# A graph network of 14 hops: the gathered edges' one-hot moves from the streaming side of the matrix product to the stationary side, in two halves of the array's columns

## What is computed

```
agg = segment_sum(h[src] * w[:, None], dst, num_segments=N)   # 14 times
out = agg @ W (+ h @ Wr) + bias ; layernorm / relu / residual
```

## Time and profile before

| what | value |
|---|---|
| time, median of 3 runs | 6878.76 us (6877.93 to 6886.88) |
| the profiled execution | 6887.01 us, span 6885.1 us |
| PE busy | 6183.2 us, 90% of the span |
| POOL busy | 4719.0 us, 69% |
| DVE busy | 2158.9 us, 31% |
| mean granted PE clock | 0.975 |

### The profile page before, as it was taken

One profiled execution on the slowest core, in us unless ns is written; L12 is line 12 of the kernel. 1 busy time (PEld: TensorE's weight loads), 2 busy tenths in 40 slices (PEclk: granted clock), 3 DMA queues, 4 the chain that ended last, 5 costly groups with the idle time before them and its releaser, 6 DMA issues.

```text
span 6885.1 us, 79487 instructions
## 1 busy us (share of the span) xinstructions
PE 6183.2 (90%) x27391; PEld 3701.9 (54%) x27592; DVE 2158.9 (31%) x8268; ACT 309.1 (4%) x843; POOL 4719.0 (69%) x4959
## 2 busy tenths in 40 slices
PE   0499752999999999989999999999999999999998
PEld 0399521655555555545655555555555555655555
DVE  8644720223322221212222233222223322222244
ACT  0000000000000000000000000000000000000000
POOL 0677777566666667667677676776767767677676
PEclk9999976999999999999999999999999999999999
DMA  9475332666666767778888888888888888888887
GB/s 359 173 310 224 97 97 77 202 195 203 181 195 184 213 199 217 218 247 288 283 290 290 294 296 288 280 286 279 296 295 289 291 286 280 285 292 291 300 295 231
DMA packets 582180, 1703.64 MB, mean 247 GB/s; under 512 B 163490, under 2 KB 325467, under 8 KB 479392
## 3 DMA queue, kind: packets, MB, share of 16 engines
q1 hardware_dynamic: 316850, 1337.88, 56.9%
q0 software_dynamic: 157584, 240.14, 12.2%
q10 hardware_dynamic: 107388, 120.98, 5.0%
HBM read 1476.43 MB, written 223.40 MB: 247 GB/s over the span
## 4 chain that ended last, share of the span: by engine, by line
PE 61%; POOL 15%; DMA 13%; issue 11%; DVE 0%; POOLq 0%; SPq 0%; ACT 0%; ACTq 0%; DVEq 0%
PE pwide L1055 33%; PE pwide L1051 16%; PE pstep L1084 9%; POOL ring_f L655 7%; POOL counts L629 6%; DMA ring_f<-table,f_src 5%; DMA counts<-lane_val,lane_idx 3%; DMA counts<-zz 3%; POOL weights L629 1%; PE pwide L1142 1%; DMA weights<-lane_val,lane_idx 1%; PE pwide L1141 0%; PE pwide L1100 0%; PE pwide L1137 0%; PE pwide L1065 0%
## 5 line engine op out<-in xcount | busy, mean ns | idle before, releaser
L655 POOL DMA_INDIRECT ring_f<-table,f_src x3492 | 3322.0, 951 | 1518.3 <-issue 916.0
L1055 PE MATMUL pwide<-room,acc 128*128 128x512 f32 (+1 forms) x3920 | 1759.0, 589 | 19.8 <-DMA room<-weights 19.8
L1055 PE MATMUL pwide<-room,hcur 128*128 128x512 f32 (+1 forms) x3136 | 1405.9, 588 | 0.0
L1084 PEld LDWEIGHTS pstep<-hot,ring_f 128*128 128x128 f32 x7272 | 1000.3, 192 | 536.0 <-issue 372.7
L1619 DVE TENSOR_SCALAR hot<-iota,f_win,f_wgt 128x64 f32<-128x64 f32 x2916 | 729.8, 334 | 1550.6 <-PE pstep L1084 1534.2
L1084 PE MATMUL pstep<-hot,ring_f 128*128 128x64 f32 x7272 | 974.1, 267 | 110.9 <-DMA ring_f<-table,f_src 109.5
L1051 PE MATMUL pwide<-room,hcur 128*128 128x512 bf16 (+1 forms) x3154 | 892.1, 367 | 187.2 <-DMA room<-counts 182.6
L1055 PEld LDWEIGHTS pwide<-room,acc 128*128 128x128 f32 x3920 | 704.5, 191 | 654.7 <-issue 604.9
L1051 PE MATMUL pwide<-room 128*128 128x512 bf16 (+1 forms) x2635 | 953.9, 367 | 2.5
L629 POOL DMA_INDIRECT counts<-lane_val,lane_idx x720 | 707.6, 983 | 220.0 <-issue 204.8
L1055 PEld LDWEIGHTS pwide<-room,hcur 128*128 128x128 f32 x3136 | 562.9, 191 | 505.3 <-issue 465.4
(11 more groups left out here) (309 smaller groups left out, 2403.2 us busy)
## 6 DMA issues: line engine op xcount, KB each, us to landing
room<-weights SPq DMA_DIRECT2D x700, 1024.0 KB
room<-counts SPq DMA_DIRECT2D x600, 512.0 KB
room<-weights SPq DMA_DIRECT2D x156, 768.0 KB
weights<-zz SPq DMA_DIRECT2D x56, 1792.0 KB
counts<-zz ACTq DMA_DIRECT2D x44, 1568.0 KB, 8.5
ring_f<-table,f_src POOLq DMA_INDIRECT x3492
room<-weights SPq DMA_DIRECT2D x56, 512.0 KB
table<-acc ACTq DMA_DIRECT2D x56, 256.0 KB
```

The source lines that it names most:

```text
L655: pool.indirect_dma_start(out=ring_f[:, slot, :], out_offset=None, in_=rows_from[:, :], in_offset=bass.IndirectOffsetOnAxis(ap=f_src[:, c: ...
L1055: ins = pe.matmul(bank[:, 0:w * P], x_of(a)[:, first + o, :], room[:, n % SLOTS, o * w * P:(o + 1) * w * P], start=begins, stop=ends)
L1084: ins = pe.matmul(bank[:, low:low + WIN], row, one, start=begins, stop=ends and not own, skip_group_check=True)
```

## The change

The operands of the gathered product change places. The one-hot (128 edges x 64 nodes) becomes stationary and fills 64 of the array's columns; the gathered rows stream (128 columns). The result stands upright, nodes x features, in the lower or the upper 64 partitions of `pstep`. The 256 nodes of a pair are four fixed blocks of 64; a chunk near an edge between blocks is used twice. So 36 steps a pair become 48 (`PLACES`), ordered so that even blocks (lower half) and odd blocks (upper half) alternate. A batch is 16 steps (`SB`) where it was 3; a pair has 3 batches; the one-hot buffer is 32 deep (two batches) where it was 27 (nine).

Since the sums are upright now, `hop1` and `hop2` scale them straight out of PSUM into the next stage's rows (ACT, `scaled_on`), and every gathered group needs a copy and a transposition before the small product (`laid`, one beat before the group's turn, which is one beat later). `lead` and `trail` become 24 and 6 in stages 1 to 4 (were 6 and 8) and 13 and -2 in the hops (were 9 and -2). The pace uses the step at which a chunk is first needed (`NEEDED`), the ring slot's wait the step at which it is used last (`LEFT`).

```diff
-STP = CHP
+EDGES_AT = ((7, 10), (15, 19), (23, 28))
+FIRST_CHUNK = [0] + [lo for lo, _ in EDGES_AT]
+END_CHUNK = [hi for _, hi in EDGES_AT] + [CHP]
+SIDES = [[(c, j) for j in (side, side + 2) for c in range(FIRST_CHUNK[j], END_CHUNK[j])] for side in range(2)]
+PLACES = [place for both in itertools.zip_longest(*SIDES) for place in both if place]
+STP = len(PLACES)
+NEEDED = [min(i for i, p in enumerate(PLACES) if p[0] >= c) for c in range(CHP)]
+LEFT = [max(i for i, p in enumerate(PLACES) if p[0] == c) for c in range(CHP)]
-HOTS = 27
+HOTS = 32
+SB = 16
-FH = 5
+FH = 0
...
-            self.turns.append(max(o[0] + 1, self.turns[-1] + GAP))
+            self.turns.append(max([o[0] + 1] + [t + GAP for t in self.turns[-1:]]) + o[1])
...
-EARLY = Split([4, 4], [4] * 10 + [1])
-LATE = Split([4, 4, 4, 4, 2], [4] * 7 + [3], 9, -2)
+EARLY = Split([4, 4], [4] * 10 + [1], 24, 6)
+LATE = Split([4, 4, 4, 4, 2], [4] * 7 + [3], 13, -2)
...
 def pace(a, c):
     p = SPLITS[a]
-    m = p.beat_of(c // HB) * p.mm // p.beats
+    m = p.beat_of((c // CHP * STP + NEEDED[c % CHP]) // SB) * p.mm // p.beats
...
-                            freed = (PAIR0[a] + pair - 1) * STP + slot
-                            pool.wait_ge(batch_done, freed // HB + 1)
+                            freed = (PAIR0[a] + pair - 1) * STP + LEFT[slot]
+                            pool.wait_ge(batch_done, freed // SB + 1)
...
+                tile, side = 2 * pair - first + block // 2, block % 2
+                sums = pstep[at % 2][side * WIN:(side + 1) * WIN, tile * P:(tile + 1) * P]
...
-                one, row = windows[:, ((BATCH0[a] + batch) * HB + n) % HOTS, :], ring_f[:, i, :]
-                ins = pe.matmul(bank[:, low:low + WIN], row, one, start=begins, stop=ends and not own, skip_group_check=True)
+                one, row = windows[:, ((BATCH0[a] + batch) * SB + n) % HOTS, :], ring_f[:, c, :]
+                ins = pe.matmul(sums, one, row, start=begins, stop=ends and not own, skip_group_check=True)
...
+            def laid(a, r):
+                at, w = SPARSE_AT[a, SPLITS[a].order[r][4]], SPLITS[a].order[r][3]
+                pe.wait_ge(upright, at + 1)
+                for j in range(w):
+                    ins = pe.transpose(pstep[at % 2][:, j * P:(j + 1) * P], z4[:, j, :], ident[:, :])
+                ins.then_inc(upright_ps, 1)
```

More of the change, by code:

```diff
@@ L46 @@
 RB = 3
-HOTS = 27
+HOTS = 32
 HB = 3
+SB = 16
 WIN = 64
-LOWS = [min(max((15 * c - 56) >> 1, 0), 2 * P - WIN) for c in range(CHP)]
 LEAD, TRAIL = 6, 8
@@ L71, in __init__ @@
         self.pairs = self.ns // 2
-        self.batches = self.pairs * STP // HB
+        self.batches = self.pairs * STP // SB
         self.mm = sum(dense) * TILES
@@ L755, in post @@
                         ins.then_inc(f_zt_done, 1)
-                    if kind in ("hop1", "hop2"):
-                        for j in range(w):
-                            ins = act.activation(x_to[:, first + j, :], t_bank[0][:, j * P:(j + 1) * P], ACT.Copy,
-                                                 scale=d2sq[:, first + j:first + j + 1])
-                        ins.then_inc(x_rdy, 1)
+                    if kind in ("hop1", "hop2") and not sparse_:
+                        scaled_on(lambda j: t_bank[0][:, j * P:(j + 1) * P])
                     if uses_h(kind):
@@ L1010, in batches @@
                         if BEAT0[a] + p.beat_of(batch) == beat:
-                            for n in range(HB):
+                            for n in range(SB):
                                 edges(a, p, batch, n)
@@ L1017, in posts @@
                         mixed(*g)
+                for g in turning(beat + 1):
+                    if SPLITS[g[0]].order[g[1]][1]:
+                        laid(*g)
                 for g in turning(beat):
@@ L1092, in turned @@
                 pe.wait_ge(z_done, G + 1)
+                if KINDS[a] == "hop2" and SPLITS[a].order[r][1]:
+                    pe.sem_inc(f_zt_ps, 1)
+                    return
                 if uses_h(KINDS[a]) and (r or KINDS[a] == 1):
@@ L1098, in turned @@
                         ins = pe.matmul(t_bank[0][:, j * D1:(j + 1) * D1], z, wc[:, :], start=True, stop=True)
-                    elif KINDS[a] not in (0, 1):
+                    elif KINDS[a] not in (0, 1) and not SPLITS[a].order[r][1]:
                         ins = pe.transpose(t_bank[0][:, j * P:(j + 1) * P], z, ident[:, :])
```

97 lines of the change are left out of this document (52 added, 45 removed).

## The result

The changed kernel takes 7236.65 us (median of 4 runs, 7233.20 to 7240.25), the kernel before in the same session 6878.35. The ratio is 1.0521, 95% interval 1.0502 to 1.0539: slower by 358 us. The forecast was 7180, in a range of 7050 to 7380.

What follows compares the result with a forecast made beforehand. PE bounds stages 1 to 4; in the hops POOL's loop and PE are nearly equal. Stages 1 to 4 +290, stage 0 -5, hops with tail +15: +300 on 6887 is 7187, as median 7180 us; range 7050 to 7380.

Steps and rivals of the forecast that it cites:

- The cost of a group on TensorE: PE, batch of 16 steps: 2.1 us, saving 7 us in each of stages 1 to 4 and 16 a hop.
- The rival in which the halves don't work side by side: PE's batches: 3.6 + 0.3 us each, hops lose 18, total 7350 us; chance 0.12.
- Waits for gathers in stages 1 to 4: PE waits 66 us a stage, as a pair's first batch wants 15 new chunks at 2.1 us each.
- The clock: Stages 1 to 4: waits lower the clock to half, eight waits at 2.4 us each, 19 us a stage.
- the lowest end of the forecast, 7060: Whole kernel: no clock term, hops unchanged, 6879 + 216 - 5 - 28.
- The hops: Nine hops: POOL's 404 us of issuing a hop stay; +12 in all, +15 with the last stage's tail.
- 4.7 a hop: End of a hop: last batch at beat 135 instead of 138, 2 more beats of dense work before the next gather.
- PE's 16 us of saving take this back and 5 more: After hop1, where PE was the later one: -5.3, so three hops sum to +4.
- So there are 25 us for PE, enough: Hops, ring slots: chunk 35 lands at 46 us, POOL wants slot 21 at 71, so no stall.
- no stall of the ring: Rival, ring stalls POOL in the hops: slot 21 late, 3 us a pair, +240, 7420 us; chance 0.06.
- Stage 5 waits for them as long as before: Start of stage 5: the 40 scatters ending stages 1 to 4 finish later with the stage, so its wait is unchanged.
- the signs named beforehand: Changed profile: ring_f waits near 65 us a stage, half clock there, stages about 470 us, hops about 432, 324 gathers in 404.

Runs made afterwards that it cites:

- run 6: Changed kernel with AHEAD_UNITS = 16 instead of 6 and trail -5 instead of -2 in the hops (last group at beat 138): 6766.06 us, ratio 0.9828.
- run 3: Changed kernel with eight steps of one column half, then eight of the other within a batch, instead of by turns: 7353.27 us, ratio 1.0709.
- Run 1: Changed kernel with a longer pace, AHEAD_UNITS = 16 instead of 6, so gathers are released earlier: 6889.94 us, ratio 1.0028.
- run 4: Changed kernel with groups of 8 steps instead of 16 (SB = 8): 6947.40 us, ratio 1.0117.
- run 11: Changed kernel, pace of 6 units, without the scatters of the hops' weights between the gathers: 6914.82 us, ratio 1.0057.
- run 7: Kernel before with only the change's later first edges (leads of 24 and 13 beats): 6812.98 us, ratio 0.9900.
- experiments 9 and 10: Run 6 with trails -3 and -4 instead of -5 in the hops (last group at beats 136 and 137): 6868.18 and 6807.77 us.
- run 9: Run 6 with trail -3 instead of -5 (last group of a hop at beat 136, dense post of 3 tiles last): 6868.18 us, ratio 0.9989.
- run 12: Kernel before with the later first edges (24 and 13 beats) and AHEAD_UNITS = 16: 6801.73 us, ratio 0.9876.
- run 2: Kernel before with AHEAD_UNITS = 16, a control: 6859.42 us, ratio 0.9984.

## Why the prediction was right, and where it was not

**The cost of a group on TensorE: right.** 2.1 us were taken, 2.06 is what the timeline of run 6 gives for a group whose halves take turns throughout (the third of a pair takes 0.2 more), and run 3 shows that the turns make it so: 3.26 us to the next dense product without them. The rival in which the halves don't work side by side is refuted. Its sum was also off: at 3.9 us a batch PE would lose 27 x 3.9 - 72.4 = 32.9 us in a hop, not 27.5, and the rival would have stood near 7400, outside the range that was to take it in.

What the Trainium skill says in "TensorEngine Tiling (Array Packing)", section Key Properties, agrees: the halves do load and multiply in parallel, and a change costs 0.38 us, though no run shows that this is a drain. What it says in "TensorE: Matmul & The Clock Gate", section The mechanism, of Part 3 on packing small matmuls, does not: here both halves use all rows, and 32 loads and matmuls still pass in 1.89 us, when eight and eight need 3.26. The measurement decides.

**Waits for gathers in stages 1 to 4: right in mechanism, a little large in size.** 66 us a stage were forecast, and 218.0 / 4 = 54.5 measured. A first group waits 9.5 on the mean and not 12 to 15, a second 3.7 and not 5. Part of the difference may be the clock, which no run separates: while it is at half, the dense work in front of a late group takes longer, so less is left to wait. Run 1 (release earlier), run 4 (fewer chunks at once) and run 11 (faster POOL) each removed one factor of the term, and in each the waits went about as the term says (to 3.8, 54.0 and 20.4 us).

**The clock: right in sign, too small.** 19 us a stage were forecast; PE's busy time fell by 127 / 4 = 32 when the waits went. That the sum came out at +278 for +290 is partly luck: the two errors are -46 and +51 for four stages, and run 7 shows another of -12, since losing the 8.4 us of waits at the start of a stage is worth 11.4, the lower clock there included. That leaves 5 us unresolved. Nor does any row give the 28 us that the lowest end of the forecast, 7060, takes off.

**The hops: this is the step that failed.** The prediction had "4.7 a hop" for the last group's earlier place, and "after hop1 ... PE's 16 us of saving take this back and 5 more", +12 in all. It was +84, and POOL's idle at the eight ends of hops holds 74 of it. The whole forecast came out 57 us too low, less than the 72 that this one term lacks. The sums over the eight ends (experiments 9 and 10) say where it went wrong:

- *The place was right.* From the last steps to the last write of the table it is 147.7 us instead of 104.7: 43, where 8 x 4.7 = 38 were forecast.
- *The way from that write to the next gather was put at nothing*, and is 55.6 instead of 27.3: 28 us. In stage 7 it is 5.3 and was 3.5, in stage 6 7.5 and was 3.1. With the place that makes the 4594.68 - 4565.26 = 29.4 us from the end of the last steps to the next gather in stage 7, where it was 4296.64 - 4275.37 = 21.3 (4275.37 is 4274.94 with the 0.43 of that row). It isn't that 3 tiles are written and not 2: run 9 writes the same 3 and has 35.4.
- *From the last gather to the end of the last steps PE was to save, and saved too little.* After hop1 it is 9.8 to 10.3 us and was 16.0 to 17.4, 6 to 7 less and not 10. At the five other ends it grew, by 22 us in all; in stage 7 it is 4565.26 - 4553.84 = 11.4, and was 6.4. PE starts the last group when it gets there (4124.10 in stage 6, 7 us after the last gather), and it gets there late: its waits for gathers in the hops are 170.7 us and not 76.1. "So there are 25 us for PE, enough" looked at the ring's slots alone. The term that I had worked out for stages 1 to 4 acts in the hops too, only weaker; that this is for want of scatters between the gathers is argued, not shown.
- So the saving of 16 us a hop did not show. PE's busy time in the hops fell by 20 us and not by 144, with the clock at 0.98 instead of 1.00, and its waits for gathers rose by 95. Run 6 has under two thirds of these waits (109.1), and there the saving is 70 us against run 12, 8 a hop. On the steps themselves, from each start to the next, it is 94 us against the kernel before; the dense and small products take 19 more.

Runs 6, 9 and 10 show what place, order and the way of the last write are worth, 126 us of the hops together (3968.8 to 3842.3), and end 37 below the kernel before.

**The small terms** held: stage 0, from its first dense product, 609.9 us for 613.5 (-4, forecast -5; the other 4 us of the table's first row lie ahead of it), 324 gathers in 403 to 407 us, no stall of the ring. "Stage 5 waits for them as long as before" holds too (17.5 us for 19.5), but run 2 shows it to be a cost that a longer pace takes away. Of the signs named beforehand, the stages of about 470 us came (465 to 470 without the step to the first hop), the hops of "about 432" did not: they are 438 to 443.

What stays open: whether SP's load just ahead of the last write is what delays it, which a run that moves only that load would tell; and why stages 1 to 4 of run 3 didn't lengthen by even the 8 us a stage that were stepped.

## What to carry to other kernels

When consumers are grouped, the wait isn't for the mean rate but for the first group's new inputs: count them, multiply by the producer's interval with all that is interleaved, and compare with the time between release and use. A throttle that was tuned for groups of 3 must be set again for groups of 16. In a loop that closes through a table, look at what posts last, what still has to be done to it, and which large loads its write meets; there a delay costs its full length in every pass, while what is saved on an engine that isn't the bound gives little.

## What the runs showed of the hardware

- Two column halves of 64 with the same 128 rows overlap when float32 steps alternate: 32 matmuls of 128 columns in 1.89 us, 3.26 when eight steps of a half stand together. The second is about the rate of single matmuls (an estimate of 0.107 for 128 columns, from 0.43 for 512), the first nearly twice that.
- A change from dense products to steps of 64 columns and back costs 0.38 us, more than three steps, by one group of 4 and one of 16. It isn't visible as idle time; it lies in the spacing of the products around it. Four matmuls with 128 stationary columns between the same dense products take 0.44 us (4133.63 to 4134.07 in the changed kernel), 0.11 each, and show no such cost.
- Waits of 1.1, 1.0 and 2.0 us, trickling through a group, were followed by 1.2 GHz (0.50 from 1521.2 to 1534.9 us), as one of 6.7 us was in the kernel before (it ends at 1394.24; the clock is 0.50 from 1389.9). In stages 1 to 4 this cost 127 us beside 214 us of waits: six tenths more on top of each microsecond waited.
- The time from a table write to the gather that it releases doesn't go by its size: 3 tiles took 8.6 us (3787.79, 3796.39 in run 1) and 3.0 (3793.94, 3796.95 in run 9), 2 tiles 5.7 (3758.43, 3764.11 in run 6) and 3.1 (3861.76, 3864.82 in the kernel before). In the two short cases SP issued no large load from 2.5 us ahead of the write to 0.7 behind it; in the two long ones it issued one 0.1 us ahead and one 0.4 behind. Which of this delays the write no run shows by itself.
